# Inverting a batch of 32x32 triangular matrices in two halves, one on VectorE and one on GpSimd

## The reference

```
q, k, v = silu(dwconv4(x @ W))            # each of the three
q, k = l2norm(q), l2norm(k);  beta = sigmoid(x @ Wb)
# 8 chunks of 32 tokens per sequence; per (sequence, head, chunk):
attn = tril(-(beta k) @ k^T, -1)          # 32x32, strictly lower
T = inv(I - attn)                         # 32x32 unit lower triangular
u = T @ (beta v);  w = T @ (beta k)
# recurrence over the 8 chunks with the state S
u_i = u - w @ S;  o_i = q @ S + local @ u_i;  S = S + k^T @ u_i
# five paths: fir3(v), fir15(v), fir64(v), o, v
# per path, token and head: mean, mean square, mean |.|, norm -> gate MLP -> softmax over the 5 paths
o = sum_p prob_p * path_p;  rmsnorm;  @ Wo
```

## Time and profile before

| | us |
|---|---|
| three runs | 455.99, 457.12, 472.33 |
| median | 457.12 |
| profiled execution, its own time | 456.23 |
| profiled execution, span from first to last instruction | 454.5 |

### The profile page before, as it was taken

How to read it: one execution, slowest core, us unless ns; L and a number is a source line. 1 busy time by engine, 2 the same in 40 slices (tenths; PEclk the granted TensorE clock), 3 DMA queues, 4 the chain that set the end, 5 groups by cost and what they waited for, 6 DMA issues and landing times.

```text
span 454.5 us, 9702 instructions
## 1 busy us (share of the span) xinstructions
PE 377.9 (83%) x4132; PEld 279.5 (61%) x4132; DVE 307.1 (68%) x461; ACT 288.2 (63%) x434; POOL 9.1 (2%) x38
## 2 busy tenths in 40 slices
PE   5599999999988976977996668936689696978996
PEld 3377776678865746855775567522256575646885
DVE  2796779547124558699979869587867696658533
ACT  4788948888267672796554317337278739457973
POOL 4000000000000010000000000000000000000000
PEclk9899999999999995698997675877689988989999
DMA  8900009200000000000700000070000000001001
GB/s 285 300 1 2 2 1 269 57 1 1 1 1 0 1 0 4 3 0 3 209 6 4 4 4 4 1 247 8 0 1 1 1 1 2 0 1 48 3 1 46
DMA packets 13428, 17.38 MB, mean 38 GB/s; under 512 B 832, under 2 KB 9024, under 8 KB 13376
## 3 DMA queue, kind: packets, MB, share of 16 engines
q1 hardware_dynamic: 13232, 16.58, 11.7%
q10 hardware_dynamic: 144, 0.01, 0.0%
HBM read 15.55 MB, written 1.05 MB: 37 GB/s over the span
## 4 chain that ended last, share of the span: by engine, by line
PE 48%; DVE 25%; ACT 16%; issue 4%; DMA 4%; SPq 1%; DVEq 0%; ACTq 0%
PE ps_a L708 11%; PE ps_a L709 11%; PE ps_a L806 4%; PE ps_a L850 4%; ACT arena L614 3%; DMA w_in<-in_w 2%; PE ps_a L895 2%; PE ps_a L862 2%; PE ps_d L773 2%; PE ps_a L893 2%; DVE acts L1084 2%; DVE arena L971 2%; PE ps_d L709 2%; PE ps_d L708 2%; DVE arena L965 2%
## 5 line engine op out<-in xcount | busy, mean ns | idle before, releaser
L708 PE MATMUL ps_a<-acts,w_f 128*128 128x512 f32 x256 | 103.7, 405 | 9.1 <-ACT acts L582 8.5
L709 PE MATMUL ps_a<-acts,w_f 128*128 128x512 f32 x256 | 101.7, 397 | 0.0
L708 PEld LDWEIGHTS ps_a<-acts,w_f 128*128 128x128 f32 x256 | 49.2, 192 | 22.6 <-ACT acts L582 10.2
L709 PEld LDWEIGHTS ps_a<-acts,w_f 128*128 128x128 f32 x256 | 49.2, 192 | 10.8 <-issue 0.7
L582 ACT ACTIVATE acts<-ps_a,vec 128x512 fp32r<-128x512 f32 x64 | 44.6, 697 | 0.0
L1103 DVE TENSOR_TENSOR acts<-gbuf,acts 128x512 fp32r<-128x512 f32 x32 | 21.6, 690 | 24.9 <-ACT acts L582 24.9
L806 PE MATMUL ps_a<-xnp,conv_w 128*128 128x512 f32 x156 | 38.3, 403 | 0.0
L965 DVE SCALAR_TENSOR_TENSOR arena<-ps_d,arena 128x512 f32<-128x512 f32 x16 | 11.0, 687 | 38.9 <-ACT arena L534 29.4
L1103 DVE TENSOR_TENSOR acts<-ghbuf,acts 128x512 fp32r<-128x512 f32 x32 | 21.2, 689 | 20.8 <-ACT acts L582 20.8
L806 PEld LDWEIGHTS ps_a<-xnp,conv_w 128*128 128x128 f32 x156 | 29.3, 188 | 8.3 <-issue 1.4
L579 ACT ACTIVATE gbuf<-ps_a,vec 128x512 f32<-128x512 f32 x32 | 22.3, 697 | 10.3 <-PE ps_a L709 10.0
(11 more groups left out here) (206 smaller groups left out, 765.5 us busy)
## 6 DMA issues: line engine op xcount, KB each, us to landing
toep<-in_fir SPq DMA_DIRECT2D x16, 288.0 KB, 5.5
w_in<-in_h SPq DMA_DIRECT2D x4, 1024.0 KB, 8.2
g_rows<-in_gW SPq DMA_DIRECT2D x4, 640.0 KB, 6.8
w_in<-in_w SPq DMA_DIRECT2D x6, 256.0 KB, 4.1
iobuf<-in_x SPq DMA_DIRECT2D x4, 256.0 KB, 6.3
toep<-in_taps SPq DMA_DIRECT2D x1, 768.0 KB, 7.0
y<-iobuf SPq DMA_DIRECT2D x3, 256.0 KB, 2.3
toep<-in_proj SPq DMA_DIRECT2D x1, 256.0 KB, 8.7
```

Of the source, the lines that this page charges most:

```text
L708: e.matmul(bank, w, hi, start=start, stop=False)
L709: return e.matmul(bank, w, lo, start=False, stop=stop)
```

## The change

The 31 steps of the substitution are made on each half apart: VectorE does half 0, GpSimd half 1 with the same two instructions per step on its own scratch. Instructions now have half the elements, and VectorE's are as many as before. VectorE does steps 0 to 10 (`SPLIT`) between the normalisations of tiles 2 and 3, steps 11 to 14 between the masks of gram 1, and the rest behind half 1's transpose. GpSimd waits for that transpose (`l_turned`) and signals its end (`pool_inv`), on which VectorE's transpose of half 1's inverse waits (`xt 1`), now just ahead of the recurrence. Half 0's window tiles, its gram and transpose, and four FIR tiles stand between the convolution tiles or ahead of gram 1; the four FIR tiles of half 1 that use filter groups 0 and 1 stand between the `aq` products, for which those groups are loaded a second time. ScalarE's evictions of windows and FIR tiles now walk in the order of the output's memory, so they read PSUM with a stride. The statistics of path (4, 1) come ahead of the recurrence, and ScalarE's scalar constants ahead of the convolution. Matrices, windows and paths have new places in the arena.

```diff
+SPLIT = 11
+FIR_ORDER = (0, 1, 4, 5, 8, 9, 12, 13, 10, 11, 14, 15, 2, 3, 6, 7)
 def att_steps():
-    for t in range(NT):
-        s.append(("qkv", 2, t))
-        if t + 2 < NT:
-            s += [("mean", 2, t + 2), ("var", 2, t + 2)]
-        if t:
-            s.append(("sumsq", 2, t - 1))
-    s += [("sumsq", 2, NT - 1), ("gram", 2, 0), ("gram", 2, 1), ("inverse", 2, 0)]
-    s += [("token", 2, i) for i in range(12)]
-    s += [("window", 2, i) for i in range(16)]
-    s += [("fir", 2, i) for i in range(12)]
+    for t in range(2):
+        s += [("qkv", 2, t), ("mean", 2, t + 2), ("window", 2, 2 * t), ("window", 2, 2 * t + 1),
+              ("var", 2, t + 2), ("sumsq", 2, t)]
+    s += [("qkv", 2, 2), ("gram", 2, 0), ("lmat", 2, 0), ("window", 2, 4), ("window", 2, 5), ("sumsq", 2, 2),
+          ("qkv", 2, 3), ("solve", 2, 0), ("window", 2, 6), ("window", 2, 7), ("sumsq", 2, 3)]
+    fir = [("fir", 2, i) for i in FIR_ORDER]
+    s += fir[0:4] + [("gram", 2, 1), ("lmat", 2, 1), ("solve", 2, 2), ("xt", 2, 0)]
+    s += [("token", 2, i) for i in (0, 1, 4, 5, 8, 9)] + fir[4:6]
+    s += [("token", 2, i) for i in (2, 3, 6, 7, 10, 11)] + fir[6:8]
+    s += [("window", 2, i) for i in range(8, 16)]
     for k in range(4):
-        s += [("yy", 2, k), ("fir", 2, 12 + k)]
+        s += [("yy", 2, k), fir[8 + k]]
...
-    s += [("sq", 2, 3), ("aq", 2, 0), ("r1", 2, 2), ("aq", 2, 1), ("r2", 2, 2), ("r3", 2, 2), ("sq", 2, 4),
-          ("aq", 2, 2), ("r1", 2, 3), ("aq", 2, 3), ("r2", 2, 3), ("r3", 2, 3)]
-    s += [("bo", 2, b) for b in range(4)] + [("sq", 2, 5)]
+    s += [("sq", 2, 3), ("aq", 2, 0), fir[12], ("r1", 2, 2), ("aq", 2, 1), fir[13], ("r2", 2, 2), ("r3", 2, 2), ("sq", 2, 4),
+          ("aq", 2, 2), fir[14], ("r1", 2, 3), ("aq", 2, 3), fir[15], ("r2", 2, 3), ("r3", 2, 3)]
+    s += [("bo", 2, b) for b in range(4)] + [("sq", 2, 5)] + sums(4) + [("sq", 2, 6), ("xt", 2, 1)]
...
# GpSimd
+            e.wait_ge(S["l_turned"], 1)
+            for j in range(DH - 1):
+                k = DH - 1 - j
+                shape = [128, k, j + 1]
+                sub = tinv[1][:, j + 1:DH, 0:j + 1]
+                prod = tmp_p[:, 0:k * (j + 1)].rearrange("p (i c) -> p i c", i=k)
+                own(e.tensor_tensor(prod, lmat[1][:, j + 1:DH, j:j + 1].to_broadcast(shape),
+                                    tinv[1][:, j:j + 1, 0:j + 1].to_broadcast(shape), ALU.mult))
+                own(e.tensor_tensor(sub, sub, prod, ALU.subtract))
+            e.memset(vec[:, 53:54], 0.0).then_inc(S["pool_inv"], 1)
...
# ScalarE, window
-                        e.activation(vt[0:WIN, :, i // 8, 4 * (i % 8):4 * (i % 8) + 4].rearrange("p c w -> p w c"),
-                                     bank[0:WIN, :].rearrange("p (w c) -> p w c", w=4), ACT.Copy
+                        e.activation(vt[i // 8][0:WIN, :, 4 * (i % 8):4 * (i % 8) + 4],
+                                     bank[0:WIN, :].rearrange("p (w c) -> p c w", w=4), ACT.Copy
```

More of the change, by code:

```diff
@@ L253, in program @@
         vpad = at("vpad", B, HIST + L)
-        vt = at("vt", 128, G, 32)
-        alt = at("alt", G, H, NCH, 3, DH)
+        vt = [at(f"vt{g}", 128, 32) for g in range(G)]
+        alt = [at("alt", G, H, NCH, 3, DH)[:, 1 - g] for g in range(G)]
         xt = at("xt", G, H, NCH, DH)
@@ L262, in program @@
                at("aq1", 4, NCH, 2, DH))
-        lmat, tinv = at("lmat", G, DH, DH), at("tinv", G, DH, DH)
-        tmp = at("tmp", 512)
-        pall = at("paths", P, G, DH, DH)
+        lmat, tinv = ([at(f"{name}{g}", DH, DH) for g in range(G)] for name in ("lmat", "tinv"))
+        tmp_d, tmp_p = (at("xt", G, DH * DH)[:, g, 0:256] for g in range(G))
+        pall = at("paths", G, P, DH, DH)[:, ::-1].rearrange("p g a t c -> p a g t c")
         paths = [pall[:, p] for p in range(P)]
@@ L816, in _ @@
                         e.wait_ge(S["dve_nrm"], NT)
-                        e.wait_ge(S["act_a"], A_AT[("qkv", 2, NT - 1)] + 3)
+                    if s == ("window", 2, 0):
                         e.wait_ge(S["pad_zero"], 1)
+                    if kind == "window" and i % 4 == 0:
+                        e.wait_ge(S["act_a"], A_AT[("qkv", 2, i // 4)] + 3)
                     bank = take_a(a)
@@ L1039, in late, with substitute @@
                                 ).then_inc(S["o_turned"], 1)
+            def substitute(first, last):
+                for j in range(first, last):
+                    k = DH - 1 - j
+                    shape = [128, k, j + 1]
+                    sub = tinv[0][:, j + 1:DH, 0:j + 1]
+                    prod = tmp_d[:, 0:k * (j + 1)].rearrange("p (i c) -> p i c", i=k)
+                    settle()
+                    own(e.tensor_tensor(prod, lmat[0][:, j + 1:DH, j:j + 1].to_broadcast(shape),
+                                        tinv[0][:, j:j + 1, 0:j + 1].to_broadcast(shape), ALU.mult))
+                    settle()
+                    own(e.tensor_tensor(sub, sub, prod, ALU.subtract))
+                if last == DH - 1:
+                    settle()
             for s in STEPS:
@@ new lines, in _ @@
+                        if i:
+                            substitute(SPLIT + h, SPLIT + h + 1)
+                elif kind == "lmat":
+                    turned = e.transpose(lmat[i].rearrange("p i j -> p (i j)"),
+                                         alt[i][:, :, :, 0, :].rearrange("p h n t -> p t (h n)"))
+                    if i:
+                        turned.then_inc(S["l_turned"], 1)
+                    else:
+                        own(turned)
+                elif kind == "solve":
+                    if i == 0:
+                        e.wait_ge(S["eye_done"], 1)
+                        substitute(0, SPLIT)
+                    else:
+                        substitute(SPLIT + H, DH - 1)
+                elif kind == "xt":
+                    if i:
+                        e.wait_ge(S["pool_inv"], 1)
+                    e.transpose(xt[:, i].rearrange("p h n t -> p t (h n)"), tinv[i].rearrange("p i j -> p (i j)")
+                                ).then_inc(S["inv_done"], 1)
```

99 lines of the change are left out of this document (41 added, 58 removed).

## The result

The changed kernel takes 454.41 us (median of 11 runs, 452.65 to 455.75). The kernel before, run beside it, took 456.12 (median of 11 runs). The ratio is 0.9954, 95% interval 0.9933 to 0.9975: faster by 0.3 to 0.7%, which is "within 2%". The forecast was 453.2. The profiled execution of the changed kernel took 455.75, at the upper end of its runs; the one of before took 456.23.

The account below looks back on a forecast made before the run. No single bound: VectorE's substitution and the TensorE/ScalarE work beside it must both shorten. Undisturbed, the recurrence starts at 240.4 instead of 253.4 us (-13.0); turns with GpSimd make it 250.4 (-3.0): 456.23 - 3.0 = 453.2, range 441 to 462.

Parts of the forecast that it names:

- Last convolution tile: TensorE's last convolution tile, with window tiles, norm products and half 0's gram moved ahead: ends at 171.4 us, before 162.3.
- Last normalisation: VectorE's last normalisation: ends at 182.4 us, 6.2 of ScalarE and 4.8 of VectorE behind 171.4, 4 us later than before.
- Gram 1 and the turn of half 1: Behind the last normalisation: gram 1 kept at 6.4 us, half 1's matrix turned at 193 us, 3 us behind the kernel before.
- VectorE's 32 instructions: Half 0's last 16 substitution steps, taking turns with GpSimd: 23.7 us, between 12.0 without cost and 29.3 in strict turns.
- Inverse of half 0: End of VectorE's substitution and transpose of half 0: there at 218.7 us with turns, 207 undisturbed, 227.1 before.
- Token, window and FIR side: TensorE and ScalarE beside the substitution, from about 190: 19 us, windows at 0.9, done at 209.7; eviction gain stays hidden.
- From the inverse to the FIR end: Four products with half 0's inverse and four FIR tiles on TensorE: 10.3 us, as before, ending at 229.5 us.
- FIR end to the recurrence: ScalarE's square, VectorE's reduces and half 1's transpose: 1.8 + 19.1 us, so the recurrence starts at 250.4 us.
- GpSimd: Half 1's 62 substitution instructions: 39 us alone, mean 0.55 to 0.62; with turns done at 235, asked for at 238.4.
- Rival (a): VectorE's substitution beside GpSimd's: no contention, the 32 steps last 12 us, kernel 443 us; chance 0.32.
- Rival (b): Steps behind half 1's turn: GpSimd costs 3.6 us per 1,000 elements, every instruction held whole; 37.6 us, kernel 467; chance 0.10.
- Rival (c): The inverse's gain goes nowhere: TensorE's low-clock gram and small matmuls keep the recurrence at 253, kernel 457 us; chance 0.08.

Follow-up runs that it names:

- e5_late_toep: Changed kernel, with the load of filter groups 2 and 3 waiting until gram 1 has ended: 449.13 us, ratio 0.9835 to the kernel before.
- e3: Changed kernel, with GpSimd's 62 substitution instructions replaced by 62 copies of 512 elements, one operand read (half 1 not inverted): 459.63 us.
- e4: Changed kernel, with GpSimd's 62 substitution instructions replaced by 12 products of 1,024 elements (half 1 not inverted): 471.57 us.
- e7_old_evict: Changed kernel, with ScalarE's window and FIR evictions in their access patterns of before: 455.94 us, ratio 1.0006 to the kernel before.
- e1_no_pool: Changed kernel, with GpSimd's 62 substitution instructions left out (half 1 not inverted): 446.34 us, ratio 0.9788 to the kernel before.
- e9: Changed kernel, with the four FIR tiles that alternate with the products with the inverse put ahead of them: 448.03 us, ratio 0.9861.
- e10: Changed kernel, with ScalarE's first two squares moved between the evictions of the products with the inverse: 452.50 us, ratio 0.9929.

## Why the prediction was right, step by step

The forecast of 453.2 and the measured 454.41 agree, a gain of 3.0 us forecast and 1.7 measured. The kind of the contention was right. That the time came out so close is luck: two steps were off by 4 to 5 us in opposite directions.

- **Last convolution tile**: forecast 171.4, measured 174.2 (164.40 + 9.76). Gram 0 started at 153.8, a microsecond ahead of the forecast 154.8, but had a 1.67-us hole and took 6.3 in place of 4.4, and the norm products took 3.30 in place of 1.9: the granted clock was 0.98 from 153 to 158 us and 0.50 behind the hole, from 158 to 162.
- **Last normalisation**: forecast 182.4, measured 184.3, so 0.9 of those 2.8 us came back: two window evictions took 1.06, not 1.8.
- **Gram 1 and the turn of half 1**: forecast 193, measured 197.9. This is the step that failed. I kept 6.4 us from the earlier trace rows and did not ask what the first FIR tiles release: SP's queue waits for exactly these, and the 2.4 MB that it then loads (8 x 288 KB) fall on gram 1. Measured 10.1 us, and 5.9 with the load moved (e5_late_toep).
- **VectorE's 32 instructions**: forecast 23.7, measured 19.3. The kind was right (turns by whole instructions, e3 and e4) and the size was not: I added up held parts of both engines, but a VectorE instruction only lasts until GpSimd's is done. Each pair took as long as the longer of the two plus a little, so 12.0 became 19.3, not 12.0 plus 11.7.
- **Inverse of half 0**: forecast 218.7, measured 219.1: the two errors, 4.9 late and 4.4 early, against each other.
- **Token, window and FIR side**: forecast 209.7, measured 212.6 (last window evicted), 2.9 later than planned with the gram 4.9 later; windows at 0.5 and not at the kept 0.9. It stayed hidden. But the same evictions in front of the last normalisation were on the path, where I had costed two windows at 1.8 us, so the gain was not all hidden as I had said: by e7_old_evict they are worth the whole gain of 0.5%.
- **From the inverse to the FIR end**: forecast 10.3, measured 12.7 (219.2 to 231.9). The first product took 1.93 us against 1.09, behind TensorE's wait of 7.55 us, at a granted clock of 0.50 (219 to 222 us), and a hole of 1.03 us stands before the last FIR piece.
- **FIR end to the recurrence**: forecast 20.9, measured 20.4. The recurrence starts at 252.2; the forecast was 250.4.
- **GpSimd**: forecast 39 us, a mean of 0.55 to 0.62; measured 38.0 us (198.16 to 236.12), means 0.516 and 0.554. Half 1's inverse was there 14 us before it was asked for.

Rival (a), no contention, is refuted by the 19.3 us of the 32 instructions, which are 12.1 in e1_no_pool. Its sum was too low besides: even without GpSimd the time is 446.3 where (a) had 443. Rival (b) is refuted by GpSimd's durations, about 1.8 us per 1,000 elements and not 3.6. Rival (c) had a true part: VectorE's wait at r3 grew from 4.45 to 8.03 us because TensorE's chain behind the inverse did not shorten (e9, e10), although the recurrence did move.

So where did 20 us of VectorE's inverse go (half 0's inverse turned at 207 undisturbed, 227.1 before)? By the runs: 7.3 to the turns with GpSimd, 4.9 to the later turn of half 1 (1.9 of them to the later normalisation, the rest to the filter load in gram 1), 2.4 to the clock and a hole behind the inverse, and about 5 to a TensorE and VectorE chain behind it that holds 3.4 us more reduces and a transpose of 2 us before the recurrence.

What stays open is why the instructions come late beside a load: whether they stand behind its data in the DMA engines or are asked for later. The trace names no engine for a packet of instructions either; that those of 16 KB are TensorE's is read from the ends of the holes. And holes are there without a load too, 1.67 us in gram 0 (packet 154.85 to 156.26, end 157.52), only shorter.

## What to carry to other kernels

Before half of a VectorE job goes to GpSimd, cost each VectorE instruction with two SBUF operands and the GpSimd instruction beside it, if that one reads SBUF, at the longer of the two. With short GpSimd instructions the split was worth 16.4 us here; twelve of 1,024 elements cost VectorE 24.5 us (36.5 against 12.0). When a step is moved forward, look at what waits for its semaphore on the DMA queues: the load it triggers moves too, and may land on small matmuls, where one wait on the queue was worth 5 us. And a wait that grows on one engine (8 us) is worth only what the next chain leaves (1.4 us).
